# A decoder layer on one core: where the second attention's inputs are loaded, how its mask enters the keys, and where its first maxima are formed

## The chip, the core and the metric

The kernel runs on one core of a Trainium2 chip. Its engines are TensorE (PE: matrix products, with PEld for the loading of their weights), VectorE (DVE), ScalarE (ACT), GpSimd (POOL) and SyncE (SP), whose queue here issues nearly all transfers. Each engine runs its own instructions in order, and engines wait for each other at semaphores. The metric is the device time of one execution in microseconds; lower is better.

## What is computed

One decoder layer on x (4 batches of 1024 tokens, 256 channels). Each of the three parts ends in a residual sum and a layer norm. The change is in the second part, the attention over a context of 77 rows for each batch.

```python
x = _layernorm(x + _L0_attn_ref(x, ...))         # attention of x on itself, rotary, alibi
# second part: q = x, k = v = ctx_1024 (4, 77, 256), 16 heads of 16 channels
qh = _split_heads(q @ Wq.T + bq)
kh = _split_heads(k @ Wk.T + bk)
vh = _split_heads(v @ Wv.T + bv)
scores = jnp.einsum('bhqd,bhkd->bhqk', qh, kh) / jnp.sqrt(jnp.float32(HEAD_DIM))
scores = scores + mask.astype(scores.dtype) * NEG          # NEG = -1e15
weights = jax.nn.softmax(scores, axis=-1)
attn = jnp.einsum('bhqk,bhkd->bhqd', weights, vh)          # then @ Wo.T + bo
# third part: a router with 8 experts, two for each token
```

## The kernel before

The program is a row of stages: projections (`stage_qkv`), first attention (`stage_attention`), its output projection with the norm and the second attention's queries (`stage_self_out`, tiles named `so_`), the second attention (`stage_cross`, tiles named `cr_`), router, experts, and the last norm. A stage begins on all engines when all have finished the one before. In a stage every engine has a program of its own, written out by hand in the order in which it runs, and semaphores tie them together. The order is fixed in the code; no planner moves anything.

Numbers are kept precise by splitting a float into two parts (hi and lo, type fp32r) and adding three products (`parts3`).

`stage_self_out` works in 8 chunks of 512 tokens. SP issues all loads first, then, chunk by chunk, the stores of x1 (`store_x1`) and of the two parts of the queries (`store_q`, to `q2_scr`).

`stage_cross` begins with a preparation:

- SP loads context, key weights, masks and constants, then the first stacks of queries. `load_stack(n)` puts the queries of chunk n, which six transfers of 256 KB read from `q2_scr`, into `qst[n % 4]`; it waits until POOL has filled that tile with ones (`pool_done`).
- ScalarE and VectorE split the context and the key weights. The parts lie in `qst[2]` and `qst[3]` (`spare`), so POOL fills these two only when the values' products are done (`turn_full` is 2).
- TensorE forms the keys for 8 pairs of heads (L1656). For each pair there are six products of 128 rows and 308 columns, and two more of one row that add the mask's parts: `mask_row` times `mask_hi` and times `mask_lo`. ScalarE and VectorE turn each result into `k_max` and `k_exp` (`key_exp`, L1380, L1474, L1476).
- Then come the maxima of the scores. A chunk has 8 half steps; `max_pairs(h)` is eight small products into `m_ps` on TensorE (L1588), and `maxima(h)` is one reduction on VectorE (L1493). There is one `m_ps`, so the products of h wait for the reduction of h-1. The first 14 (`LEAD`) run ahead of everything else, with the values' products (L1667) behind h = 1.
- When a chunk's eight maxima are there, `shifts(n)` negates them, `transpose_top(n)` turns them on TensorE, `copy_top(n)` copies them (ScalarE), and `move_top(n)` on SP writes them to `shift_scr` and reads them back into two rows of the query stack (`top_in`). `scores(n, 0)` waits for that. SP's order at the start is `load_stack(0)`, `load_stack(1)`, `load_x(0)`, `load_stack(2)`, `move_top(0)`, `load_stack(3)`, `move_top(1)`.

The main loop then runs over the 8 chunks: in each of a chunk's 8 steps the maxima of a later chunk, the scores of this one, and pieces of values, transposes, projection and norm of this and earlier chunks.

Of the kernel before, what the change touches and what calls it, by code (L numbers as in the profile page):

```python
# [12 lines left out]
F32 = mybir.dt.float32  # L13
# [892 lines left out]
def stage_self_out(nc, io):  # L906

    with Scope(nc, "so") as s:
# [5 lines left out]
        ident = s.sb("ident", [P, P], F32)  # L914
# [35 lines left out]
        def _(sp):  # L950
# [192 lines left out]
L = 77  # L1143
# [46 lines left out]
def stage_cross(nc, io):  # L1190


    with Scope(nc, "cr") as s:
# [7 lines left out]
        ctx = s.sb("ctx", [P, CK, B * L], F32)  # L1201
        wk_raw = s.sb("wk_raw", [P, CK, C], F32)
        wv_raw = s.sb("wv_raw", [P, CK, C], F32)
        bk = s.sb("bk", [P, PAIRS], F32)
        kinds = s.sb("kinds", [P, 3], F32)
        bv = s.sb("bv", [P, C], F32)
        mask_raw = s.sb("mask_raw", [1, P], F32)
        mask_row = s.sb("mask_row", [1, P], F32R)
        mask_i = s.sb("mask_i", [1, B * L], I32)
        mask_f = s.sb("mask_f", [1, B * L], F32)  # L1210
        mask_hi = s.sb("mask_hi", [1, B * L], F32R)
        mask_lo = s.sb("mask_lo", [1, B * L], F32R)
        key_i = s.sb("key_i", [L, B], I32)
        key_bias = s.sb("key_bias", [L, B], F32)
        wo_raw = s.sb("wo_raw", [P, CK, C], F32)
        wo_hi = s.sb("wo_hi", [P, CK, C], F32R)
        wo_lo = s.sb("wo_lo", [P, CK, C], F32R)
        bo = s.sb("bo", [P, C], F32)
        ident = s.sb("ident", [P, P], F32)
# [13 lines left out]
        s_ps = [s.pb(f"s_ps{i}") for i in range(S_BANKS)]  # L1233
# [11 lines left out]
        ctx_in, wv_in = s.sem("ctx_in"), s.sem("wv_in")  # L1245
        const_in, late_in = s.sem("const_in"), s.sem("late_in")
# [24 lines left out]
        def key_bank(j):  # L1271

            banks = [x[:, :] for x in s_ps] + [a_ps[:, :], m_ps[:, 0, :], m_ps[:, 1, :]] + [x[:, :] for x in turn_ps]
            return banks[j][:, 0:B * L]

# [5 lines left out]
        def _(sp):  # L1281
# [35 lines left out]
            sp.dma_start(ctx[:, :, :], io["ctxT"].rearrange("(c p) n -> p c n", p=P)).then_inc(ctx_in, 16)  # L1317
            sp.dma_start(wk_raw[:, :, :], io["wkT"].rearrange("(c p) n -> p c n", p=P)).then_inc(ctx_in, 16)
            sp.dma_start(mask_i[:, :], io["mask"]).then_inc(const_in, 16)
            sp.dma_start(mask_raw[:, :], io["mask_row"]).then_inc(const_in, 16)  # L1320
# [1161 lines left out]
```

## Time and profile before

| | |
|---|---|
| median of 3 runs | 1915.79 us (1911.1 to 1917.71) |
| time of the profiled execution | 1916.35 us |
| its span, first to last instruction | 1914.6 us |
| busy share of the span: PE, DVE, ACT, POOL | 86%, 68%, 52%, 21% |
| mean granted TensorE clock | 0.906 of full |

The profile covers one execution. A busy share is a mean over stages with different limits, so a change in one stage has to be read in that stage: which engine waits there, for whom, and when. A clock of 1.00 is 2.4 GHz and 0.50 is 1.2 GHz. The second attention takes from about 1037 to about 1297 us in this execution.

### The profile page before, as it was taken

The numbers are of one execution on the slowest core, as the hardware profiler recorded it, in microseconds if no ns is written. First come the engines' busy times: TensorE is split into PE (matmuls) and PEld (weight loads), VectorE is DVE, ScalarE is ACT, GpSimd is POOL, SyncE is SP. The second block draws the span as 40 slices with busy tenths as digits, with TensorE's granted clock in tenths as the row PEclk, the third lists the DMA queues.
The fourth block names the chain that finished last, engine by engine and source line by source line (L and its number), as shares of the span: only waits on it lengthen the run. The fifth ranks groups of instructions, "written<-read, shape, count | busy, mean of one in ns | idle before, by whom it ended". The sixth has DMA issues, their size and how long they took to land. (4 is left out here: it accounts for less than half of the span.)

```text
span 1914.6 us, 36288 instructions
## 1 busy us (share of the span) xinstructions
PE 1654.9 (86%) x14824; PEld 1080.1 (56%) x14824; DVE 1296.4 (68%) x2288; ACT 992.3 (52%) x1692; POOL 404.2 (21%) x268
## 2 busy tenths in 40 slices
PE   7858999999999999998584799877993999999970
PEld 7734444444444444443374555545762888988870
DVE  6687888888888888883294446752333777777736
ACT  5324777777777777777342166853442333333310
POOL 6440000000000000000223100000453344444430
PEclk9957999999999999999797567977996999999995
DMA  7877444444444444400546766313213233334225
GB/s 254 218 186 210 63 68 65 66 66 68 67 66 65 69 63 68 64 14 8 182 143 179 111 94 112 80 45 133 90 41 113 67 92 92 92 92 92 37 31 178
DMA packets 131409, 183.93 MB, mean 96 GB/s; under 512 B 30904, under 2 KB 95560, under 8 KB 130188
## 3 DMA queue, kind: packets, MB, share of 16 engines
q1 hardware_dynamic: 117804, 159.56, 39.4%
q0 software_dynamic: 13440, 22.07, 5.5%
q8 instruction: 117, 1.92, 0.5%
q14 instruction: 48, 0.39, 0.1%
HBM read 114.95 MB, written 69.99 MB: 97 GB/s over the span
## 5 line engine op out<-in xcount | busy, mean ns | idle before, releaser
L638 DVE TENSOR_REDUCE att_row_max<-att_ring 128x2 f32<-128x1024 f32 x512 | 602.4, 1220 | 108.0 <-PE att_ring L704 56.9
L622 ACT ACTIVATE att_w_exp<-att_s_ps 128x512 f32<-128x512 f32 x1024 | 547.8, 596 | 231.9 <-PE att_s_ps L747 156.4
L774 PE MATMUL att_a_ps<-att_w_exp,att_v_group 128*32 128x512 f32 x2048 | 273.6, 606 | 0.2 <-ACT att_w_exp L622 0.2
L733 PE MATMUL att_s_ps<-att_q_stack,att_k_stack 62*128 62x512 f32 x640 | 181.5, 480 | 0.0
L733 PEld LDWEIGHTS att_s_ps<-att_q_stack,att_k_stack 62*128 62x128 f32 x640 | 84.3, 184 | 123.9 <-ACT att_w_exp L622 112.8
L2156 ACT ACTIVATE ex_hid<-ex_h_ps,ex_b 128x512 f32<-128x512 f32 x128 | 87.2, 686 | 116.4 <-DVE ex_h_lo L2211 66.6
L2112 POOL DMA_INDIRECT x_scr<-ex_y,ex_home x64 | 106.7, 1666 | 181.4 <-DVE ex_y L2201 166.8
L560 POOL COPY att_eyes<-keep_slope_eye 128x384 bf16<-128x384 bf16 x16 | 8.1, 507 | 641.1 <-PE att_s_ps L747 631.8
L2211 DVE TENSOR_TENSOR ex_h_lo<-ex_hid,ex_h_hi 128x512 fp32r<-128x512 f32 x128 | 138.8, 1085 | 4.4
L704 PE MATMUL att_ring<-att_k_stack,att_q_stack 60*128 60x512 f32 x640 | 131.4, 451 | 6.3 <-DVE att_att L665 3.2
L747 PE MATMUL att_s_ps<-att_eyes,keep_past_bf 64*128 64x64 bf16 x3840 | 133.4, 193 | 0.0
L733 PE MATMUL att_s_ps<-keep_q_stack,keep_k_stack 62*128 62x512 f32 x384 | 114.3, 488 | 8.9 <-ACT att_w_exp L622 6.3
L747 PEld LDWEIGHTS att_s_ps<-att_eyes,keep_past_bf 64*128 64x128 bf16 x3840 | 93.6, 96 | 30.0 <-issue 13.5
L704 PE MATMUL att_ring<-keep_k_stack,keep_q_stack 60*128 60x512 f32 x384 | 89.8, 503 | 22.2 <-DVE att_row_max L638 11.2
L733 PEld LDWEIGHTS att_s_ps<-keep_q_stack,keep_k_stack 62*128 62x128 f32 x384 | 51.6, 188 | 88.9 <-ACT att_w_exp L622 80.3
L1402 ACT ACTIVATE cr_e<-cr_s_ps,cr_key_bias 77x512 f32<-77x512 f32 x128 | 80.3, 679 | 31.1 <-PE cr_s_ps L1608 30.1
L1817 POOL DMA_INDIRECT rows_scr<-ro_x_send,ro_put_u x64 | 64.8, 1013 | 123.3 <-DVE ro_put_u L1930 69.0
L2142 ACT ACTIVATE ex_x_hi<-ex_t_ps 128x1024 fp32r<-128x1024 f32 x16 | 16.4, 1027 | 141.1 <-PE ex_t_ps L2260 141.1
L1493 DVE TENSOR_REDUCE cr_top<-cr_m_ps 128x8 f32<-128x616 f32 x64 | 51.0, 797 | 53.8 <-PE cr_m_ps L1588 53.7
L2209 DVE CAST ex_h_hi<-ex_hid 128x512 fp32r<-128x512 f32 x128 | 72.7, 568 | 14.5 <-ACT ex_hid L2156 13.5
L2219 DVE TENSOR_TENSOR ex_y<-ex_y_ps,ex_b 128x256 f32<-128x256 f32 x64 | 25.4, 421 | 81.8 <-PE ex_y_ps L2283 81.8
L2283 PE MATMUL ex_y_ps<-first_w_hi,ex_h_lo 128*128 128x256 f32 x256 | 72.5, 283 | 0.0
(296 smaller groups left out, 3544.0 us busy)
## 6 DMA issues: line engine op xcount, KB each, us to landing
first_w_raw<-ew SPq DMA_DIRECT2D x16, 1024.0 KB
att_k_stack<-qk_scr SPq DMA_DIRECT2D x120, 128.0 KB
cr_q_stack<-q_scr SPq DMA_DIRECT2D x48, 256.0 KB, 9.3
keep_k_stack<-qk_scr SPq DMA_DIRECT2D x72, 128.0 KB
rows_scr<-att_zeros POOLq DMA_DIRECT2D x8, 1040.0 KB, 22.0
ex_rows<-rows_scr SPq DMA_DIRECT2D x16, 520.0 KB
att_q_stack<-qk_scr SPq DMA_DIRECT2D x60, 128.0 KB
qk_scr<-qkv_t_hi SPq DMA_DIRECT2D x7, 1024.0 KB, 4.3
```

The costliest lines, as they stand in the source:

```text
L622: nc.scalar.activation(w_exp[(STEPS * g.n + st) % SETS][h][:, :], s_ps[v % BANKS][:, :], ACT.Exp).then_inc(exp_done, 1)
L638: nc.vector.tensor_reduce(out, ring[place.slot][:, :, :], AX.X, ALU.max).then_inc(ring_free, 1)
L704: return nc.tensor.matmul(ring[place.slot][:, i, :], qs[g.buf][rows, j, tok:tok + P], ks[g.buf][rows, half, j, kk * CH:(kk + 1) * CH], sta ...
L733: ins = nc.tensor.matmul(s_ps[v % BANKS][:, :], ks[g.buf][rows, c, j, kt * P:(kt + 1) * P], qs[g.buf][rows, j, c * CH:(c + 1) * CH], start ...
L747: ins = nc.tensor.matmul(s_ps[bank][:, at:at + 64], past[side, far, half, :], eyes[g.buf][side, part, h // 2, :], start=False, stop=n == last)
L774: ins = nc.tensor.matmul(a_ps[32 * h:32 * h + 32, :], vg[g.buf][:, kt, h * VW:h * VW + 32], w_exp[(STEPS * g.n + st) % SETS][h][:, :], sta ...
L1402: nc.scalar.activation(e[p % E_SETS][:, side, :], s_ps[v % S_BANKS][0:L, :], ACT.Exp, bias=key_bias[:, n // 2:n // 2 + 1]).then_inc(exp_do ...
L2112: pool.indirect_dma_start(io["x2_scr"], bass.IndirectOffsetOnAxis(home[h % 4][:, t, :], 0), y[c][:, t, :], None, compute_op=ALU.add).then_ ...
L2156: nc.scalar.activation(hid[m % 2][:, :], h_ps[m % 2][:, :], ACT.Relu, bias=b1[:, bass.ds(e, 1), m:m + 1].rearrange("p a b -> p (a b)") if ...
L2209: nc.vector.tensor_copy(h_hi[c][:, m, :], hid[m % 2][:, :]).then_inc(h_hi_done, 1)
L2211: nc.vector.tensor_tensor(h_lo[c][:, m, :], hid[m % 2][:, :], h_hi[c][:, m, :].bitcast(F32), ALU.subtract).then_inc(h_lo_done, 1)
L2283: ins = nc.tensor.matmul(y_ps[t][:, 0:C], a, b, start=(j == 0), stop=(j == len(prods) - 1))
```

## The change

There are three edits.

1. A scope `pre` holds context, weights, biases, masks, constants and the identity for both stages. `load_cross` issues their 11 transfers in `stage_self_out`, behind the loads of that stage's eighth chunk and ahead of its first store. `stage_cross` issues none of them (it issued twelve), and waits for one semaphore, `cross_in`.
2. `mask_hi` and `mask_lo` become one tile of 64 rows, `mask_parts`: the high part in row 0, the low part in row 32, zeros elsewhere, as in `mask_row`. The two products of one row become one of 64 rows.
3. The first 14 maxima alternate between `m_ps` and the first two score banks (`max_bank`), and wait for the reduction two before.

```diff
@@ stage_self_out, SP
             for n in range(1, CHUNKS):
                 load(n)
+            load_cross(sp, io, pre)
             for n in range(CHUNKS + 2):
@@ new
+def load_cross(sp, io, pre):
+
+    for tile, name in (("ctx", "ctxT"), ("wk_raw", "wkT"), ("wv_raw", "wvT"), ("wo_raw", "woT")):
+        sp.dma_start(pre[tile][:, :, :], io[name].rearrange("(c p) n -> p c n", p=P)).then_inc(pre["cross_in"], 16)
+    for tile, name in (("bk", "bk_stack"), ("kinds", "kinds"), ("mask_raw", "mask_row"), ("mask_i", "mask"), ("key_i", "maskT")):
+        sp.dma_start(pre[tile][:, :], io[name]).then_inc(pre["cross_in"], 16)
+    for name in ("bv", "bo"):
+        sp.dma_start(pre[name][:, :], io[name].partition_broadcast(P)).then_inc(pre["cross_in"], 16)
@@ stage_cross
-        s_ps = [s.pb(f"s_ps{i}") for i in range(S_BANKS)]
+        score_ps = s.pb("score_ps", (P, S_BANKS, 512))
+        s_ps = [score_ps[:, i, :] for i in range(S_BANKS)]
+        def max_bank(h):
+
+            return score_ps[:, 0:2, :] if h < LEAD and h % 2 else m_ps[:, :, :]
@@ SP
-            sp.dma_start(ctx[:, :, :], io["ctxT"].rearrange("(c p) n -> p c n", p=P)).then_inc(ctx_in, 16)
...
             load_stack(0)
-            sp.dma_start(wv_raw[:, :, :], io["wvT"].rearrange("(c p) n -> p c n", p=P)).then_inc(wv_in, 16)
-            sp.dma_start(bv[:, :], io["bv"].partition_broadcast(P)).then_inc(wv_in, 16)
-            sp.dma_start(ident[:, :], io["ident"]).then_inc(late_in, 16)
             load_stack(1)
-            sp.dma_start(bo[:, :], io["bo"].partition_broadcast(P)).then_inc(late_in, 16)
-            sp.dma_start(wo_raw[:, :, :], io["woT"].rearrange("(c p) n -> p c n", p=P)).then_inc(late_in, 16)
             load_x(0)
@@ VectorE
-            nc.vector.tensor_copy(mask_hi[:, :], mask_f[:, :]).then_inc(prep, 1)
+            nc.vector.tensor_copy(mask_parts[:, :], mask_f[:, :]).then_inc(prep, 1)
             dve.wait_ge(prep, 7)
-            nc.vector.tensor_tensor(mask_lo[:, :], mask_f[:, :], mask_hi[:, :].bitcast(F32), ALU.subtract).then_inc(prep, 1)
+            nc.vector.tensor_tensor(mask_parts[32:64, :], mask_f[32:64, :], mask_parts[32:64, :].bitcast(F32), ALU.subtract).then_inc(prep, 1)
@@ TensorE
-                if h:
+                if 2 <= h < LEAD:
+                    pe.wait_ge(m_free, h - 1)
+                elif h >= LEAD:
                     pe.wait_ge(m_free, h)
-                prods += [(mask_row[:, :], x[:, :]) for x in (mask_hi, mask_lo)]
+                prods.append((mask_row[:, :], mask_parts[:, :]))
```

The next two lists are TensorE's rows at the end of the key products and the start of the maxima, before and then after. `q_stack` here stands for the split context and weights, which lie in that tile's memory; each row gives the result's shape and the number of like instructions.

```order
L1656 MATMUL cr_turn_ps<-cr_q_stack 128x308 x6
L1656 MATMUL cr_turn_ps<-cr_mask_hi,cr_mask_row 128x308
L1656 MATMUL cr_turn_ps<-cr_mask_lo,cr_mask_row 128x308
L1588 MATMUL cr_m_ps<-cr_k_max,cr_q_stack 128x78 x16
L1667 MATMUL cr_turn_ps<-cr_q_stack 77x256 x24
L1588 MATMUL cr_m_ps<-cr_k_max,cr_q_stack 128x78 x56
L1597 MATMUL cr_turn_ps<-cr_ident,cr_neg 32x128 x4
```

```order
L1666 MATMUL cr_turn_ps<-cr_q_stack 128x308 x6
L1666 MATMUL cr_turn_ps<-cr_mask_parts,cr_mask_row 128x308
L1598 MATMUL cr_m_ps<-cr_k_max,cr_q_stack 128x78 x8
L1598 MATMUL cr_score_ps<-cr_k_max,cr_q_stack 128x78 x8
L1677 MATMUL cr_turn_ps<-cr_q_stack 77x256 x24
L1598 MATMUL cr_m_ps<-cr_k_max,cr_q_stack 128x78 x8
L1598 MATMUL cr_score_ps<-cr_k_max,cr_q_stack 128x78 x8
```

Each pair of heads has one product less, and the groups of eight maxima products now alternate between two tiles. The order of the groups is the same.

The next two lists are SP's rows at the start of the second attention, before and then after. In the kernel before, seven loads (context, key weights, masks, constants) stand ahead of the first row.

```order
L1292 DMA cr_q_stack<-q_scr 16x8x512 x6
L1325 DMA cr_wv_raw<-wvT 128x2x256
L1326 DMA cr_bv<-bv 128x256
L1327 DMA cr_ident<-ident 128x128
L1292 DMA cr_q_stack<-q_scr 16x8x512 x6
L1329 DMA cr_bo<-bo 128x256
L1330 DMA cr_wo_raw<-woT 128x2x256
L1299 DMA cr_x<-x_scr 128x4x256
L1292 DMA cr_q_stack<-q_scr 16x8x512 x6
L1304 DMA shift_scr<-cr_neg_t 32x512
L1308 DMA cr_q_stack<-shift_scr 2x4096 x2
```

```order
L1315 DMA cr_q_stack<-q_scr 16x8x512 x12
L1322 DMA cr_x<-x_scr 128x4x256
L1315 DMA cr_q_stack<-q_scr 16x8x512 x6
L1327 DMA shift_scr<-cr_neg_t 32x512
L1331 DMA cr_q_stack<-shift_scr 2x4096 x2
```

The weights and constants are gone from this place, and the third stack still stands ahead of the write to `shift_scr`.

## Rows read from the trace of the kernel before

**Rows 1.** The page's first line: span and instructions.

```profile
span 1914.6 us, 36288 instructions
```

**Rows 2.** Busy time in one stretch: PE, PEld, DVE, ACT, POOL, PEclk, DMA share, GB/s.

```profile
1050.00:1055.00 5.00, 5.00 (x16) 3.76 (x16) 0.00 (x0) 0.00 (x0) 0.00 (x0) 0.50 1.07 122
```

**Rows 3.** Timeline (start, length, engine, line, operation): SP's loads and stores, then stage_cross.

```profile
952.17 1.42 SPq L953 DMA_DIRECT2D so_x<-x  x1
...
964.17 0.37 SPq L957 DMA_DIRECT2D x_scr<-so_x  x1
...
1042.06 0.80 DVE L1451 TENSOR_TENSOR cr_q_stack<-cr_ctx,cr_q_stack 128x616 fp32r<-128x616 f32 x1 [1.11 <-ACT cr_q_stack L1362]
...
1046.45 1.88 PE L1656 MATMUL cr_s_ps<-cr_q_stack 128*128 128x308 f32 x6 [18.65 <-DVE cr_mask_row L1467]
```

**Rows 4.** Timeline, TensorE, the second key product, then the first maxima product.

```profile
1049.07 0.63 PE L1656 MATMUL cr_s_ps<-cr_q_stack 128*128 128x308 f32 x1
...
1049.49 0.97 PE L1656 MATMUL cr_s_ps<-cr_q_stack 128*128 128x308 f32 x3
...
1050.51 0.46 PE L1656 MATMUL cr_s_ps<-cr_q_stack 128*128 128x308 f32 x1
...
1050.90 0.62 PE L1656 MATMUL cr_s_ps<-cr_mask_hi,cr_mask_row 1*128 1x308 f32 x1
...
1051.71 0.63 PE L1656 MATMUL cr_s_ps<-cr_q_stack 128*128 128x308 f32 x1
...
1069.48 1.08 PE L1588 MATMUL cr_m_ps<-cr_k_max,cr_q_stack 52*128 52x78 f32 x8 [1.82 <-DVE cr_k_max L1476]
```

**Rows 5.** Timeline, TensorE, maxima products and what follows them.

```profile
1088.16 1.07 PE L1588 MATMUL cr_m_ps<-cr_k_max,cr_q_stack 52*128 52x78 f32 x8 [0.98 <-DVE cr_top L1493]
...
1089.17 1.03 PE L1597 MATMUL cr_turn_ps<-cr_ident,cr_neg 128*32 128x128 f32 x4
...
1100.64 1.07 PE L1588 MATMUL cr_m_ps<-cr_k_max,cr_q_stack 52*128 52x78 f32 x8 [1.55 <-DVE cr_wo_lo L1538]
...
1101.49 0.72 PE L1608 MATMUL cr_s_ps<-cr_q_stack,cr_k_exp 50*77 50x512 f32 x2
```

**Rows 6.** Timeline, the maxima before and behind the values' products.

```profile
1071.45 1.08 PE L1588 MATMUL cr_m_ps<-cr_k_max,cr_q_stack 52*128 52x78 f32 x8 [0.89 <-DVE cr_top L1493]
...
1077.02 0.64 PE L1588 MATMUL cr_m_ps<-cr_k_max,cr_q_stack 52*128 52x78 f32 x8
...
1087.22 0.80 DVE L1493 TENSOR_REDUCE cr_top<-cr_m_ps 128x8 f32<-128x616 f32 x1 [1.17 <-PE cr_m_ps L1588]
```

**Rows 7.** Timeline of POOL and SP's queue, one busy stretch, transfers' landing (last: shift_scr's).

```profile
1077.15 6.97 POOL L1350 MEMSET cr_q_stack<- 128x4096 f32 x2 [32.85 <-PE cr_turn_ps L1667]
...
1080.69 2.70 SPq L1292 DMA_DIRECT2D cr_q_stack<-q_scr  x6
...
1090.85 0.31 SPq L1304 DMA_DIRECT2D shift_scr<-cr_neg_t  x1
...
1096.18 0.54 SPq L1308 DMA_DIRECT2D cr_q_stack<-shift_scr  x2
...
1093.00:1094.00 1.00, 0.18 (x2) 0.03 (x2) 0.78 (x1) 0.00 (x0) 0.00 (x0) 0.50 0.66 72
...
cr_wv_raw<-wvT SPq DMA_DIRECT2D x1, 256.0 KB, 12.8
...
DMA to landing us min/median/max: 1.6/3.7/7.0
```

**Rows 8.** Timeline, ScalarE, copy_top of successive chunks; busy time in two stretches.

```profile
1150.34 0.59 ACT L1393 ACTIVATE cr_neg_t<-cr_turn_ps 32x512 fp32r<-32x512 f32 x1 [1.50 <-PE cr_turn_ps L1597]
...
1178.46 0.59 ACT L1393 ACTIVATE cr_neg_t<-cr_turn_ps 32x512 fp32r<-32x512 f32 x1 [1.70 <-PE cr_turn_ps L1597]
...
1198.84 0.59 ACT L1393 ACTIVATE cr_neg_t<-cr_turn_ps 32x512 fp32r<-32x512 f32 x1 [1.49 <-PE cr_turn_ps L1597]
...
1165.00:1170.00 5.00, 5.00 (x31) 2.43 (x28) 1.50 (x3) 2.77 (x5) 0.00 (x0) 0.50 1.08 144
```

More of the change, by code:

```diff
@@ L903, in chunk_rows, with cross_tiles, stage_self_out @@
     return ap.rearrange("(n t p) e -> n p t e", p=P, t=TPC)[n]
-def stage_self_out(nc, io):
+CROSS_LOADS = 11
+MASK_ROWS = 64
+def cross_tiles(s):
+    shapes = {"ctx": [P, CK, B * L], "wk_raw": [P, CK, C], "wv_raw": [P, CK, C], "wo_raw": [P, CK, C], "bk": [P, PAIRS],
+              "bv": [P, C], "bo": [P, C], "kinds": [P, 3], "mask_raw": [MASK_ROWS, P], "ident": [P, P]}
+    pre = {name: s.sb(name, shape, F32) for name, shape in shapes.items()}
+    pre["mask_i"], pre["key_i"] = s.sb("mask_i", [MASK_ROWS, B * L], I32), s.sb("key_i", [L, B], I32)
+    pre["cross_in"] = s.sem("cross_in")
+    return pre
+def load_cross(sp, io, pre):
[5 more added lines that the diff above has]
+        sp.dma_start(pre[name][:, :], io[name].partition_broadcast(P)).then_inc(pre["cross_in"], 16)
+L = 77
+def stage_self_out(nc, io, pre):
     with Scope(nc, "so") as s:
@@ L1187, with stage_cross @@
 TURNS = turns()
[L1190 removed]
+def stage_cross(nc, io, pre):
     with Scope(nc, "cr") as s:
@@ L1271, in key_bank @@
         def key_bank(j):
-            banks = [x[:, :] for x in s_ps] + [a_ps[:, :], m_ps[:, 0, :], m_ps[:, 1, :]] + [x[:, :] for x in turn_ps]
+            banks = s_ps + [a_ps[:, :], m_ps[:, 0, :], m_ps[:, 1, :]] + [x[:, :] for x in turn_ps]
             return banks[j][:, 0:B * L]
+        def max_bank(h):
+            return score_ps[:, 0:2, :] if h < LEAD and h % 2 else m_ps[:, :, :]
         def exp_lag(p):
@@ L1587, in max_pairs @@
                         rows = slice(64 * side, 64 * side + ROWS_MAX)
-                        ins = nc.tensor.matmul(m_ps[:, side, j * LP:(j + 1) * LP], q[rows, first + j, t * P:(t + 1) * P],
+                        ins = nc.tensor.matmul(max_bank(h)[:, side, j * LP:(j + 1) * LP], q[rows, first + j, t * P:(t + 1) * P],
                                                k_max[rows, first + j, b, :], start=True, stop=True)
@@ L2367, in consts @@
         "kinds": kinds.astype(f),
-        "mask_row": mask[None, :].astype(f),
+        "mask_row": padded_rows(mask[None, :].astype(f)),
         "before": (a[:, None] < a[None, :]).astype(f),
@@ L2386, in stacked_bk, with padded_rows @@
     return out.reshape(P, PAIRS)
+def padded_rows(a):
+    out = np.zeros((MASK_ROWS, a.shape[1]), a.dtype)
+    out[::MASK_ROWS // 2] = a
+    return out
 def padded_rw2(w):
@@ L2400 @@
     "ctxT": ("ctx_1024", lambda a: a.reshape(B * L, C).T),
-    "mask": ("mask_Bx1x1xS2_ik0", lambda a: a.reshape(1, B * L)),
+    "mask": ("mask_Bx1x1xS2_ik0", lambda a: padded_rows(a.reshape(1, B * L))),
     "maskT": ("mask_Bx1x1xS2_ik0", lambda a: a.reshape(B, L).T),
@@ L2455, in build @@
             stage_attention(nc, io, keep)
-        stage_self_out(nc, io)
-        stage_cross(nc, io)
+        with Scope(nc, "pre") as c:
+            pre = cross_tiles(c)
+            stage_self_out(nc, io, pre)
+            stage_cross(nc, io, pre)
         with Scope(nc, "first") as w:
```

47 lines of the change are left out of this document (13 added, 34 removed).

## The prediction

> **What bounds the kernel now.** I read the page first for its span [rows 1]. The profiled execution took 1916.35 us, 1.75 us more than that span, and lies 0.56 us above the median of the runs shown. I take the sum from 1916.35 us and carry it over to the median. The page's chain of waits covers only the last norm, so it says nothing of the second attention. There I read the timeline engine by engine, then the busy time in short stretches, then the transfers.
>
> The reader should see four things. First, in the key products TensorE is busy 5.00 us of 5.00, at half clock [rows 2]: this phase is bound by TensorE. Second, in the first maxima TensorE and VectorE take turns: from one group of eight products to the next are 1.97 us (1069.48 to 1071.45), with 0.89 us of TensorE waiting for VectorE [rows 4, 6]. Third, the first scores run at 1101.49, right behind the fifteenth maxima, which waited 1.55 us for the low part of the output weights [rows 5]. Fourth, the stage has another chain towards those scores. POOL fills `qst[2]` when the values' products are done, SP then loads that stack, and the write of the first maxima to `shift_scr` stands behind it in the same queue [rows 7].
>
> **The start of the stage.** VectorE waited 1.11 us for ScalarE's part of the context, which waited for the load [rows 3]. With the load done in the stage before, that wait goes. VectorE's own steps (fills, splits, mask) then follow without a gap, so TensorE's first key product moves from 1046.45 to 1045.34: **1.11 us**. The mask steps keep their 308 columns on 64 rows in place of one, which I cost at nothing, since a wider partition range adds no columns. ScalarE's later wait for the value bias goes too; it caught up before the last key, so I give it nothing.
>
> **The moved transfers.** By their shapes they are 1.33 MB (308 KB, three times 256, two times 128, five small ones), in 11 transfers. SP issued the last load of `stage_self_out` at 952.17 and the first store at 964.17, 10.6 us after that load's issue ended [rows 3]. The slowest rate in the rows is 256 KB in 12.8/6 = 2.1 us (the six stack transfers ahead of the value weights, [rows 7]), which would make 5.2 x 2.13 = 11.1 us. So they fit or push the first store by about 1 us, and the first to wait for that store is VectorE two chunks later. I take 0. If that cover were gone, at most these 11.1 us would come back once. Five issues fewer ahead of the second stack matter little: stack 0 waits for POOL's fill anyway.
>
> **The mask product.** One pair of heads takes 1051.71 - 1049.07 = 2.64 us [rows 4]. Between full products the distance is (1050.51 - 1049.49)/4 = 0.255 us. The first one takes 0.42 (1049.07 to 1049.49), the sixth 0.39, and the two products of one row 0.81 together (1050.90 to 1051.71). So one row costs no less than 128, and each change of height costs about 0.15 at either side. Removing one product removes at least 0, if the one of 64 rows took the whole 0.81. It removes 0.855 if it fits in like a full one. Which of the two is it nearer to? Eight maxima products of 52 rows take 0.85 us when the scores of 50 rows follow (1100.64 to 1101.49), but 1.01 when transposes of 128 rows follow (1088.16 to 1089.17) [rows 5]. So a product of half height pays the change as the one-row product does. I take one streaming time, 0.255 us for each pair: 8 x 0.255 = **2.04 us**. The first maxima product moves from 1069.48 to 1066.33.
>
> **The two places.** h = 1 starts 0.86 us behind h = 0 rather than 1.97, so it gives **1.11 us** more, and the values' products follow. The maxima behind them start at 1077.02 - 4.26 = 1072.76 [rows 6]. Two groups then share a cycle of 1.97 us, 0.985 each, so the reduction of h = 7 ends near 1072.76 + 5 x 0.985 + 1.9 = 1079.6, against 1088.02 (87.22 + 0.80) before: 8.4 us earlier [rows 6]. h = 14 and the output weights' low part would let the scores go near 1087.3, or 14.2 us earlier. That is what the maxima alone would give.
>
> **What is late next.** The scores also need the maxima's round trip. POOL's fill of `qst[2]` hangs on the values' products, so it moves only by 4.26 us, from 1077.15 to 1072.9 [rows 7]. The third stack's loads go from 1080.69 to 1076.4. Before, their traffic ended inside 1093 to 1094 (0.66 busy), and the write issued at 1090.85 had landed by 1096.18. The value weights, issued right behind six such transfers, landed 12.8 us after their issue: the queue is served in order. Now the write is issued near 1082.4, 8.4 us earlier, but six transfers that end near 1089.4 are ahead of it. It lands at 1096.18 - 4.26 = 1091.9. The read back then takes between 1.6 us (the least of these transfers' landings [rows 7]) and 5.3 (before, the scores started that long after its issue [rows 5, 7]). I take 2.7 us, an estimate nearer to the least, as the queue is then empty; the median is 3.7 with stacks in the way. Scores start near 1094.6 in place of 1101.49: **6.9 us** earlier, with ends of 4.3 and 8.0. On SP, the third and fourth stack and every later round trip stand behind this wait. They move by 4.3 us or more and were not late before. On TensorE, everything of the main loop is queued behind the scores. So about 7 of the 14 us are lost in a wait for `top_in`, some 7 us long.
>
> Sum: 1916.35 - 6.9 = 1909.4 us, or 1908.9 on the median's basis; I say 1909.
>
> **Rivals.**
>
> *A product of 64 rows is free of the change of height.* It saves 0.855 us for each pair, 4.8 us more in all, ahead of the values' products, and so ahead of both chains: 1904.6. For it speaks only that no such product stands among full ones in the trace; against it the 0.16 us of [rows 5]. Chance 0.13.
>
> *The clock rises in the key products.* If it does at the middle, four pairs save 1.2 us each and the values about 1 us: 5.8 us more, 1903.6. Against it, TensorE was busy 5.00 of 5.00 and the granted clock stayed at 0.50, 1.2 GHz [rows 2]; for it, that six products of seven are now full, where it was six of eight. Chance 0.05. The Trainium skill (TensorE: Matmul & The Clock Gate, "What's actually happening") says that the gate follows how busy TensorE has been of late, and that activity releases it. By that rule alone the clock would have risen in this phase already, before the change as behind it; the row disagrees.
>
> *The write does not wait for the third stack.* Then the two places pay in full, 14.2 us: 1902. Against it stands the order seen in [rows 7]. Chance 0.07.
>
> *Slower: the clock in the main loop.* The place is chunks 1 to 4 of the loop. From the second `copy_top` row to the third are 20.4 us; the chunk ahead of it, which holds a stretch at 0.50 with TensorE busy all of it, took 28.1 [rows 8]. One such chunk more costs 7.7 us, and whether the clock rises in a chunk may hang on how its work falls in time, which the change moves. At 0.9 chunk the gain is gone (1909.4 + 6.9), from 1.6 on the kernel is slower by more than 0.3%; two give 1924.8. As easily, the chunk that ran at half before is spared, and the time is 1901.7. The three runs lie within 6.6 us, which speaks against large swings. Chance of slower this way 0.12.
>
> *The change does little.* If the read back takes 5.3 us and the mask product saves nothing, 2.3 us are left: 1914. Chance 0.1.
>
> **How the numbers follow.** The forecast has 0.53. Its own range is 1905 to 1913, by the round trip's ends and part of a clock stretch. About 0.3%, 5.7 us, is what a measurement of this kernel can tell from no change, so the forecast lies just beyond that bound, and some 0.19 of its 0.53 falls inside. The three rivals with larger gains hold 0.25, of which I count 0.24 as faster; the little gain counts as the same. Together: faster 0.58, same 0.30, slower 0.12. The range for 8 in 10 reaches over the other gains to 1901 and over the small gain to 1917.
>
> **What would show it.** Right: TensorE's first key product 1.1 us nearer to the stage's start; 2.39 us for a pair of heads; maxima groups 0.98 us apart; then TensorE idle for about 7 us, ended by the landing of `shift_scr`'s read; the write's landing about 9.5 us after its issue. Wrong: 1.8 us for a pair, a clock of 1.00 before the values, a write that lands within 4 us of its issue, or a chunk of the main loop of 28 us that was of 20.

## The result: 1905.38 us, 0.55% less than before

Over eight executions of each, the changed kernel takes 1905.38 us (median; 1900.54 to 1910.79) and the kernel before 1915.45 (1911.1 to 1918.45). The ratio is 0.9945, with a 95% interval of 0.9927 to 0.9963: a small gain, clear of noise. The forecast was 1909, with a range of 1901 to 1917. The profiled execution took 1905.45 us, against 1916.35: 10.9 us less.

The page of the changed kernel begins with this line, the counterpart of [rows 1]:

```profile
span 1903.6 us, 36270 instructions
```

**Where the 10.9 us are.** In POOL's and SP's timeline (start, length, engine, line, operation), POOL's first fill marks the start of `stage_cross` and SP's first load of the router its end. After the change:

```profile
1040.52 6.96 POOL L1361 MEMSET cr_q_stack<- 128x4096 f32 x2 [4.67 <-POOLq L49]
...
1070.16 6.96 POOL L1361 MEMSET cr_q_stack<- 128x4096 f32 x2 [22.68 <-PE cr_turn_ps L1677]
...
1077.09 2.34 POOL L1368 TENSOR_TENSOR cr_x<-cr_x,pre_bo 128x1024 f32<-128x1024 f32 x1
...
967.60 15.66 SPq L985 DMA_DIRECT2D x_scr<-so_x  x3
...
1073.69 2.67 SPq L1315 DMA_DIRECT2D cr_q_stack<-q_scr  x6
...
1081.25 0.32 SPq L1327 DMA_DIRECT2D shift_scr<-cr_neg_t  x1
...
1090.07 0.54 SPq L1331 DMA_DIRECT2D cr_q_stack<-shift_scr  x2
...
1286.80 0.35 SPq L1798 DMA_DIRECT2D ro_ident<-ident  x1
```

And the same two marks in the kernel before:

```profile
1037.34 6.96 POOL L1350 MEMSET cr_q_stack<- 128x4096 f32 x2 [4.68 <-POOLq L49]
...
1297.71 0.35 SPq L1788 DMA_DIRECT2D ro_ident<-ident  x1
```

The stage took 1297.71 - 1037.34 = 260.37 us and takes 1286.80 - 1040.52 = 246.28 now: 14.1 less. It starts 3.2 us later; already the end of the first stage, which the change does not touch, is 2.85 us later in this execution. What follows the stage is alike: 1914.6 - 1297.71 = 616.9 us and 1903.6 - 1286.80 = 616.8. `stage_self_out` did not grow: from its first store of x1 ([rows 3] and 967.60 here) to the stage's start are 73.17 us before and 72.92 now. So its own work hides the 11 transfers.

**Inside the stage**, all times from POOL's first fill. TensorE's timeline of the changed kernel, which answers to [rows 4 to 6]:

```profile
1049.32 1.88 PE L1666 MATMUL cr_score_ps<-cr_q_stack 128*128 128x308 f32 x6 [18.33 <-DVE cr_mask_row L1475]
...
1051.68 1.91 PE L1666 MATMUL cr_score_ps<-cr_q_stack 128*128 128x308 f32 x6
...
1054.07 1.91 PE L1666 MATMUL cr_score_ps<-cr_q_stack 128*128 128x308 f32 x6
...
1058.63 1.12 PE L1666 MATMUL cr_m_ps<-cr_q_stack 128*128 128x308 f32 x6
...
1060.01 1.12 PE L1666 MATMUL cr_m_ps<-cr_q_stack 128*128 128x308 f32 x6
...
1066.04 0.64 PE L1598 MATMUL cr_m_ps<-cr_k_max,cr_q_stack 52*128 52x78 f32 x8 [1.82 <-DVE cr_k_max L1484]
...
1066.51 0.62 PE L1598 MATMUL cr_score_ps<-cr_k_max,cr_q_stack 52*128 52x78 f32 x8
...
1067.06 3.04 PE L1677 MATMUL cr_turn_ps<-cr_q_stack 128*77 128x256 f32 x24
...
1070.02 0.64 PE L1598 MATMUL cr_m_ps<-cr_k_max,cr_q_stack 52*128 52x78 f32 x8
...
1087.10 1.07 PE L1598 MATMUL cr_m_ps<-cr_k_max,cr_q_stack 52*128 52x78 f32 x8 [1.55 <-DVE cr_wo_lo L1546]
...
1094.90 0.71 PE L1618 MATMUL cr_score_ps<-cr_q_stack,cr_k_exp 50*77 50x512 f32 x2 [6.73 <-DMA cr_q_stack<-shift_scr]
```

| | before | after | change |
|---|---|---|---|
| first key product | 9.11 | 8.80 | -0.31 |
| first maxima (h = 0) | 32.14 | 25.52 | -6.62 |
| maxima of h = 2, behind the values | 39.68 | 29.50 | -10.18 |
| write of the first maxima issued | 53.51 | 40.73 | -12.78 |
| first scores | 64.15 | 54.38 | -9.77 |
| end of the stage | 260.37 | 246.28 | -14.09 |

One pair of heads takes 1054.07 - 1051.68 = 2.39 us at first; at 1058.63 its six full products take 1.12 us in place of 1.91, and the whole pair 1060.01 - 1058.63 = 1.38. Busy time in stretches (length, PE, PEld, DVE, ACT, POOL, clock, DMA share, GB/s) shows why, beside [rows 2]:

```profile
1050.00:1055.00 5.00, 5.00 (x16) 3.84 (x16) 1.40 (x3) 1.04 (x2) 0.00 (x0) 0.50 1.05 127
...
1060.00:1065.00 5.00, 4.22 (x22) 3.14 (x21) 4.06 (x8) 3.61 (x8) 0.00 (x0) 1.00 1.06 132
```

TensorE is busy 5.00 of 5.00 as before, and the granted clock goes from 0.50 (1.2 GHz) to 1.00 (2.4 GHz) inside the key products. In the kernel before it stayed at 0.50 through all of them and rose only in the values' products.

VectorE has two surprises, its cast of the mask and the two steps of `shifts(0)`, which negate the first maxima. The first line is a step that is as quick as before:

```profile
1044.01 0.76 DVE L1459 TENSOR_TENSOR cr_q_stack<-pre_ctx,cr_q_stack 128x616 fp32r<-128x616 f32 x1
...
1046.48 1.17 DVE L1467 CAST cr_mask_f<-pre_mask_i 64x308 f32<-64x308 int32 x1
...
1070.80 0.79 DVE L1501 TENSOR_REDUCE cr_top<-cr_m_ps 128x8 f32<-128x616 f32 x1
...
1074.58 0.79 DVE L1501 TENSOR_REDUCE cr_top<-cr_score_ps 128x8 f32<-128x616 f32 x1
...
1075.41 1.76 DVE L1508 TENSOR_SCALAR cr_neg<-cr_top 128x64 fp32r<-128x64 f32 x1
...
1077.20 2.30 DVE L1510 SCALAR_TENSOR_TENSOR cr_neg<-cr_top,cr_neg 128x64 fp32r<-128x64 f32 x1
```

The same steps before the change:

```profile
1044.61 0.30 DVE L1459 CAST cr_mask_f<-cr_mask_i 1x308 f32<-1x308 int32 x1
...
1088.05 0.19 DVE L1500 TENSOR_SCALAR cr_neg<-cr_top 128x64 fp32r<-128x64 f32 x1
...
1088.28 0.23 DVE L1502 SCALAR_TENSOR_TENSOR cr_neg<-cr_top,cr_neg 128x64 fp32r<-128x64 f32 x1
```

The six reductions of h = 2 to 7 now follow each other (1070.80 to 1074.58, 0.76 us each, against a cycle of 1.97 before [rows 4, 6]). But `shifts(0)` takes 4.09 us from its first step's start to its second's end, in place of 0.46.

Behind the scores the loop is the same code, yet it takes 191.90 us in place of 196.22. Two successive `copy_top` rows of ScalarE's timeline, beside [rows 8]:

```profile
1124.50 0.59 ACT L1401 ACTIVATE cr_neg_t<-cr_turn_ps 32x512 fp32r<-32x512 f32 x1 [1.73 <-PE cr_turn_ps L1607]
...
1150.42 0.59 ACT L1401 ACTIVATE cr_neg_t<-cr_turn_ps 32x512 fp32r<-32x512 f32 x1 [1.50 <-PE cr_turn_ps L1607]
```

These are the third and fourth, 25.9 us apart. The chunk of 28.1 us in [rows 8] lay one later; that place takes 20.4 us now.

### The profile page after: what moved, and what is told of

It reads as the page before. It is cut to its first block and busy times, and to the rows that moved or that the text cites. A ratio compares the mean times of both kernels' runs of the same rounds, so it can differ in the third digit from the quotient of the medians.

```text
span 1903.6 us, 36270 instructions
## 1 busy us (share of the span) xinstructions
PE 1637.1 (86%) x14816; PEld 1066.9 (56%) x14816; DVE 1302.4 (68%) x2288; ACT 993.9 (52%) x1692; POOL 403.4 (21%) x268
## 5 line engine op out<-in xcount | busy, mean ns | idle before, releaser
L704 PE MATMUL att_ring<-keep_k_stack,keep_q_stack 60*128 60x512 f32 x384 | 89.8, 503 | 22.2 <-DVE att_row_max L638 11.2
L1410 ACT ACTIVATE cr_e<-cr_score_ps,cr_key_bias 77x512 f32<-77x512 f32 x128 | 80.3, 678 | 30.0 <-PE cr_score_ps L1618 29.1
L1501 DVE TENSOR_REDUCE cr_top<-cr_m_ps 128x8 f32<-128x616 f32 x57 | 45.4, 797 | 45.6 <-PE cr_m_ps L1598 45.3
L1846 ACT ACTIVATE ro_hid<-ro_h_ps,ro_rb 128x512 f32<-128x512 f32 x64 | 44.0, 687 | 60.5 <-PE ro_h_ps L1980 60.5
```

The lines of the kernel that those rows point to most:

```text
L704: return nc.tensor.matmul(ring[place.slot][:, i, :], qs[g.buf][rows, j, tok:tok + P], ks[g.buf][rows, half, j, kk * CH:(kk + 1) * CH], sta ...
L1410: nc.scalar.activation(e[p % E_SETS][:, side, :], s_ps[v % S_BANKS][0:L, :], ACT.Exp, bias=key_bias[:, n // 2:n // 2 + 1]).then_inc(exp_do ...
```

## The experiments

Three sets of four kernels ran, each set beside the kernel before on the same chip. A ratio is to that. The points in time in the table come from one profiled execution of each kernel and are again from the stage's start; "trip" is from the issue of the write of the first maxima to the first scores.

| kernel | h = 0 | h = 2 | write | scores | trip | scores to end | ratio, 95% |
|---|---|---|---|---|---|---|---|
| before | 32.14 | 39.68 | 53.51 | 64.15 | 10.64 | 196.22 | 1 |
| the changed kernel | 25.52 | 29.50 | 40.73 | 54.38 | 13.65 | 191.90 | 0.9945 |
| again, first set | 28.53 | 35.46 | 46.68 | 59.26 | 12.58 | 196.46 | 0.9927 [0.9900, 0.9954] |
| again, second set | 28.45 | 35.35 | 46.58 | 58.48 | 11.90 | 194.97 | 0.9956 [0.9922, 0.9991] |
| again, third set | 24.34 | 29.83 | 41.05 | 51.85 | 10.80 | 194.70 | 0.9941 [0.9922, 0.9961] |
| mask in two products | 31.71 | 38.90 | 50.12 | 62.31 | 12.19 | 191.88 | 0.9991 [0.9965, 1.0016] |
| one place | 23.38 | 30.84 | 44.67 | 55.46 | 10.79 | 191.41 | 0.9970 [0.9948, 0.9993] |
| one place, repeated | 24.42 | 32.27 | 45.97 | 56.60 | 10.63 | 189.74 | 0.9956 [0.9935, 0.9977] |
| early loads alone | 31.71 | 39.34 | 53.16 | 63.80 | 10.64 | 196.00 | 1.0001 [0.9982, 1.0020] |
| mask product alone | 28.84 | 36.37 | 50.19 | 60.83 | 10.64 | 196.08 | 0.9987 [0.9962, 1.0011] |
| mask added twice | 25.61 | 32.61 | 43.84 | 55.19 | 11.35 | 191.90 | 0.9954 [0.9922, 0.9987] |
| spare tiles swapped | 24.25 | 29.74 | 37.75 | 48.56 | 10.81 | 195.03 | 0.9914 [0.9891, 0.9937] |
| trip on ScalarE's queue | 24.52 | 30.04 | 41.27 | 59.21 | 17.94 | 194.79 | 0.9984 [0.9954, 1.0013] |
| the same, one place | 28.51 | 36.06 | 49.89 | 67.78 | 17.89 | 191.45 | 0.9991 [0.9963, 1.0019] |

**The changed kernel again.** The same code; it also serves as the measure for its set.

> The changed kernel once more. Theory A (the 64-row mask product lets the clock rise in the key products every time): the granted clock goes from 0.50 to 1.00 inside the eight key products here as well, the first maxima product starts 25 to 26 us behind the stage's first instruction, and the time is 10 us below the kernel before. Theory B (the clock rose there by chance of timing): the clock may stay at 0.50 through all key products, first maxima 28 to 29 us behind the stage's start, and the time is some 5 us below the kernel before. In both TensorE waits 6 to 8 us for shift_scr's read ahead of the first scores.

1904.04 us. The clock rose in the key products again, but only 24.8 us behind the stage's start in place of 17.8, which puts h = 0 3 us later (28.53; neither theory had that), and the main loop took 4.6 us more. The profiled execution was the slowest of its seven, 1913.44 us. So the time of the rise and the loop's length are properties of an execution, and differences of 3 to 5 us between two profiles say nothing of the code. The medians and counts over kernels have to.

**The mask in two products of one row**, the rest as changed:

```diff
-        mask_parts = s.sb("mask_parts", [MASK_ROWS, B * L], F32R)
+        mask_hi = s.sb("mask_hi", [1, B * L], F32R)
+        mask_lo = s.sb("mask_lo", [1, B * L], F32R)
...
-                prods.append((mask_row[:, :], mask_parts[:, :]))
+                prods += [(mask_row[0:1, :], x[:, :]) for x in (mask_hi, mask_lo)]
```

> The changed kernel with two mask products of one row as before; loads and two places stay. Theory A: pairs of heads at 2.64 us, clock at 0.50 through all of them, first maxima product 30.5 us behind the stage's start (25.5 in the changed kernel), and since the third stack hangs on it the first scores 5 to 7 us later: time 5 to 7 us above the changed kernel. Theory B: the clock rises or not as in the changed kernel; the time is 2 us above it.

1912.87 us, 8.8 us above the changed kernel of its set, and the two intervals do not touch. TensorE's timeline, first maxima and first scores:

```profile
1070.60 1.07 PE L1599 MATMUL cr_m_ps<-cr_k_max,cr_q_stack 52*128 52x78 f32 x8 [1.82 <-DVE cr_k_max L1485]
...
1101.20 0.71 PE L1619 MATMUL cr_score_ps<-cr_q_stack,cr_k_exp 50*77 50x512 f32 x2 [5.27 <-DMA cr_q_stack<-shift_scr]
```

The clock stayed at 0.50 through the key products, as before, and h = 0 starts 6.2 us later than in the changed kernel. 8 x 0.255 = 2.04 us of this is the shorter work; the rest is the clock.

**One place for the first maxima**, the rest as changed:

```diff
-            return score_ps[:, 0:2, :] if h < LEAD and h % 2 else m_ps[:, :, :]
+            return m_ps[:, :, :]
...
-                if 2 <= h < LEAD:
-                    pe.wait_ge(m_free, h - 1)
-                elif h >= LEAD:
-                    pe.wait_ge(m_free, h)
+                if h:
+                    pe.wait_ge(m_free, h)
```

> The changed kernel with all first maxima in m_ps again; loads and the mask product stay. Theory A (the maxima's round trip through shift_scr sets the first scores): the maxima behind the values' products take 1.5 to 2 us each in place of 0.8 to 1, the 13th ends some 6 to 10 us later, but the scores begin at most 2 to 3 us later, since they waited 6.7 us for the read; time 1 to 3 us above the changed kernel. Rival (the maxima set it): 6 to 10 us above it.

1911.36 us, 7.3 us above the changed kernel of its set: by the medians the rival's figure. In the profiles its scores come only 1.1 us later than in the changed kernel, as theory A has it, so the two measures disagree. Here is TensorE's row of the first scores, which wait for nothing:

```profile
1094.62 0.71 PE L1616 MATMUL cr_score_ps<-cr_q_stack,cr_k_exp 50*77 50x512 f32 x2
```

**Both undone**, so that only the early loads are left:

> The kernel before with the early loads alone (two one-row mask products, one place). My sum: 0.3 to 1.1 us below the kernel before, not to be told from it. Rival (late loads of the value bias and weights held ScalarE and so the keys): 4 us or more below it.

1916.61 us, ratio 1.0001, with an interval of 0.2% to either side: no worth or cost of the early loads alone can be seen.

**The round trip on ScalarE's queue.** `move_top(0)` leaves SP's order; ScalarE issues its write and its read behind `copy_top(0)`. The aim was to take the trip out from behind the third stack.

```diff
             load_stack(2)
-            move_top(0)
...
             copy_top(0)
+            act.wait_ge(top_copied, 1)
+            nc.scalar.dma_start(io["shift_scr"][0], neg_t[0][:, :].bitcast(F32)).then_inc(top_out, 16)
+            act.wait_ge(top_out, 16)
+            for side in range(2):
+                row = 64 * side + ROW_SHIFT
+                nc.scalar.dma_start(qst[0][row:row + 2, :, :].bitcast(F32), ...).then_inc(top_in[0], 16)
```

> The changed kernel, but the first chunk's round trip through shift_scr (one write, two reads) is issued by ScalarE on its own queue, not by SP behind the third stack. Theory A (the trip waits in SP's queue behind the third stack): the read is issued within 4 us of the write (8.2 to 8.8 in the changed kernel), the first scores start 3 to 7 us earlier, then the maxima of step 16 wait for the third stack instead; time 2 to 5 us below the changed kernel. Rival (transfers share the engines whatever the queue, or the maxima set the pace): the read is issued as late as before, time unchanged.

1912.41 us (0.9984 [0.9954, 1.0013]): not to be told from the kernel before, nor, by the intervals, from the changed kernel on the same chip (0.9956 [0.9922, 0.9991]). ScalarE's issues and TensorE's first scores:

```profile
1078.37 0.35 ACTq L1425 DMA_DIRECT2D shift_scr<-cr_neg_t  x1
...
1089.84 0.73 ACTq L1429 DMA_DIRECT2D cr_q_stack<-shift_scr  x2
...
1096.31 0.71 PE L1624 MATMUL cr_score_ps<-cr_q_stack,cr_k_exp 50*77 50x512 f32 x2 [11.02 <-DMA cr_q_stack<-shift_scr]
```

The write took 11.5 us to the read's issue and the read 6.5. SP, no longer held by the trip, issued the twelve transfers of the third and fourth stack one behind the other from 1070.81 on, ahead of the write. So a queue of another engine gave this write no way past twelve transfers: the theory that the order within SP's queue alone makes the write late fell. The run doesn't show what the write would take there with only six ahead.

**The same, with one place.**

> As e5, but with all first maxima in m_ps. Theory A: now that the trip is short, the maxima's own pace shows: first scores 4 to 8 us later than in e5, and no earlier than in e3 by more than 1 us. Rival (the two places are worth little anyway): within 2 us of e5.

1915.35 us (0.9991 [0.9963, 1.0019]), scores at 67.78 against 59.21. The clock rose 9 us later in this profile, which puts h = 0 4 us later (28.51 against 24.52), so only about half of the 8.6 us is the maxima's. The times don't tell the two apart. The write took 12.6 us to the read's issue here.

**The mask added twice**, by two products of 64 rows. This tells "fewer products" from "another height":

```diff
-                prods.append((mask_row[:, :], mask_parts[:, :]))
+                prods += [(mask_row[:, :], mask_parts[:, :])] * 2
```

> The changed kernel with the 64-row mask product done twice for each pair (the mask is added twice). A pair takes 2.64 us at half clock, as in the kernel before. Theory A1 (two products in eight that use few rows kept the clock low): it rises here too, since half the rows are in use, and the first maxima come 24 to 30 us behind the stage's start. Theory A2 (it is the share of full products, six of eight or six of seven): the clock stays at 0.50, first maxima at 31.7 us as with the one-row products, and the time is 4 to 8 us above the changed kernel.

1906.26 us. TensorE's timeline of the key products:

```profile
1049.42 0.88 PE L1666 MATMUL cr_score_ps<-cr_mask_parts,cr_mask_row 64*128 64x308 f32 x2
...
1050.23 1.91 PE L1666 MATMUL cr_score_ps<-cr_q_stack 128*128 128x308 f32 x6
...
1052.88 1.65 PE L1666 MATMUL cr_score_ps<-cr_q_stack 128*128 128x308 f32 x6
...
1056.45 1.11 PE L1666 MATMUL cr_m_ps<-cr_q_stack 128*128 128x308 f32 x6
...
1064.42 1.07 PE L1598 MATMUL cr_m_ps<-cr_k_max,cr_q_stack 52*128 52x78 f32 x8 [1.82 <-DVE cr_k_max L1484]
```

A pair takes 1052.88 - 1050.23 = 2.65 us at half clock, as much as before with one-row products (2.64 [rows 4]), and six of its eight products are full, as before. Yet the clock rose: its six full products take 1.65 us in the third pair and 1.11 in the fifth. So the share of full products doesn't decide it, and the rows in the two mask products do. The work of a pair is no shorter here than before the change, and still the ratio is 0.9954: that points to the clock, not the spared product, as what the mask edit is worth.

**The changed kernel, second and third time.**

> The changed kernel once more, on the same chip as e5 to e7: clock up inside the key products, first maxima 25 to 29 us behind the stage's start, first scores at 54 to 60 us, waiting 5 to 7 us for the read of shift_scr; 8 to 13 us below the kernel before.

1908.98 us. The clock rose at 24.7 us, and the scores waited 4.98 us for the read.

> The changed kernel as reference on this chip: 8 to 13 us below the kernel before, clock up inside the key products, first scores 54 to 60 us behind the stage's start.

1903.67 us. The clock rose at 14.9 us, and the scores came at 51.85 us, 2 us before the earliest that was expected. SP's queue and TensorE's first scores, the measure for the next kernel:

```profile
1069.34 2.67 SPq L1315 DMA_DIRECT2D cr_q_stack<-q_scr  x6
...
1076.89 0.32 SPq L1327 DMA_DIRECT2D shift_scr<-cr_neg_t  x1
...
1083.71 0.54 SPq L1331 DMA_DIRECT2D cr_q_stack<-shift_scr  x2
...
1087.69 0.71 PE L1618 MATMUL cr_score_ps<-cr_q_stack,cr_k_exp 50*77 50x512 f32 x2 [3.88 <-DMA cr_q_stack<-shift_scr]
```

**The spare tiles swapped.** The parts of context and key weights change places with those of the value weights, so that `qst[2]` comes free with the keys (`k_done`), 7 us before the values are done:

```diff
-        ... for i in (2, 3)]
+        ... for i in (3, 2)]
...
                 if i == 2:
+                    pool.wait_ge(k_done, PAIRS)
+                if i == 3:
                     pool.wait_ge(turn_full, 2)
```

> The changed kernel with the two borrowed stacks exchanged: the split key weights lie in qst[2], context and value weights in qst[3], and POOL fills qst[2] when the key products are done, not when the values' products are. Theory A (the third stack's loads and the round trip behind them set the first scores): the third stack's load is issued some 5 to 7 us earlier relative to the first maxima (as far as the earlier stacks' traffic allows), the read lands and the first scores start 1 to 6 us earlier than in e11, more where the clock rose late; time 1 to 5 us below e11. Rival (the maxima set the pace): no change against e11.

1898.97 us (1894.98 to 1904.01), the fastest of all, 16 us below the kernel before. It is 4.7 us below the changed kernel of its set, with six executions of each and intervals that overlap, so this last step is likely and not certain. The timeline of POOL, VectorE, SP and TensorE:

```profile
1059.08 3.51 POOL L1363 MEMSET cr_q_stack<- 128x4096 f32 x1 [15.53 <-PE cr_turn_ps L1668]
...
1069.93 2.35 POOL L1370 TENSOR_TENSOR cr_x<-cr_x,pre_bo 128x1024 f32<-128x1024 f32 x1
...
1071.70 0.63 DVE L1510 TENSOR_SCALAR cr_neg<-cr_top 128x64 fp32r<-128x64 f32 x1
...
1072.37 0.23 DVE L1512 SCALAR_TENSOR_TENSOR cr_neg<-cr_top,cr_neg 128x64 fp32r<-128x64 f32 x1
...
1062.62 2.79 SPq L1315 DMA_DIRECT2D cr_q_stack<-q_scr  x6
...
1074.34 0.32 SPq L1327 DMA_DIRECT2D shift_scr<-cr_neg_t  x1
...
1080.37 0.54 SPq L1331 DMA_DIRECT2D cr_q_stack<-shift_scr  x2
...
1085.15 0.71 PE L1620 MATMUL cr_score_ps<-cr_q_stack,cr_k_exp 50*77 50x512 f32 x2 [3.89 <-DMA cr_q_stack<-shift_scr]
```

The third stack's load goes out 26.0 us behind the stage's start in place of 33.5, and the scores come 3.3 us earlier, which is what the chain through the third stack had led one to expect. But the rows say that the 3.3 us were won ahead of the trip. The trip takes as long as in its twin (1074.34 to 1085.15 is 10.81 us; 1076.89 to 1087.69 above is 10.80). The write is issued 3.3 us earlier, because `shifts(0)` takes 0.90 us in place of 4.10.

**One place, repeated,** beside its own measure of the changed kernel:

> e3 once more beside the changed kernel. Theory A (round trip sets the first scores, the second place gives only the 1.1 us at h = 1): time within 2 us of e11. Rival (the two places are worth what e3's median said): 4 to 7 us above e11.

1904.53 us against 1903.67: within the noise. The 7 us of the first comparison did not come back. In the profiles its scores come 4.8 us later and its main loop is 5.0 us shorter, so the stage is as long in both (246.34 and 246.55 us). One thing is steady: from h = 0 to the scores it is 32.0 to 32.2 us in all five profiles with one place in which SP makes the trip, and 27.5 to 30.7 in the six with two places in the common order of tiles. The second place thus brings the scores 1.3 to 4.7 us nearer to h = 0.

**The mask product alone,** on the kernel before:

> The kernel before with the mask edit alone. Theory A (the mask product lets the clock rise, and the late value bias then holds ScalarE): the clock rises inside the key products, ScalarE starts its first k_high near 20.6 us behind the stage's start, where the value bias lands, and the eight pairs then take 1.09 us each, so the first maxima come at 29 to 31 us (32.1 before; 23.4 to 28.5 with loads and mask); time 1 to 4 us below the kernel before. Rival (loads do nothing whatever the clock): first maxima at 24 to 29 us and time as in e10.

1911.23 us (0.9987 [0.9962, 1.0011]). ScalarE's split of the value weights, and TensorE's last pair:

```profile
1053.80 0.63 ACT L1369 ACTIVATE cr_q_stack<-cr_wv_raw 128x512 fp32r<-128x512 f32 x1 [12.49 <-DMA cr_bv<-bv]
...
1060.80 1.12 PE L1656 MATMUL cr_turn_ps<-cr_q_stack 128*128 128x308 f32 x6
```

The split waits 12.49 us for the load of the value bias, which this kernel issues in the stage. Even so the clock rose in the key products, at 25.1 us, at the end of the seventh pair, and h = 0 comes at 28.84. The wait for the value bias can hardly be the reason for the late rise: with early loads it came as late in three profiles (24.7 to 24.8 us), with h = 0 at 28.45 to 28.53.

## Why `shifts(0)` and the casts became slow

The timelines, laid side by side, show it. In the changed kernel POOL's second fill ends at 1070.16 + 6.96 = 1077.12, and the first step of `shifts(0)` at 1075.41 + 1.76 = 1077.17. POOL's next step, a sum on `cr_x`, runs from 1077.09 to 1079.43, and the second step of `shifts(0)` ends at 1079.50. The mask's cast ends at 1046.48 + 1.17 = 1047.65 in the profile, just behind POOL's first fill (1047.48). It is so in every one of the fourteen profiles:

| | VectorE's step meets POOL's | VectorE's step comes later |
|---|---|---|
| mask's cast against POOL's first fill | 1.17 or 1.18 us in 12 profiles (all with early loads; it starts 1.0 before the fill's end in each) | 0.30 us in 2 (before, mask product alone; 0.2 to 0.3 behind its end) |
| `shifts(0)`, first and second step, against POOL's second fill and sum | 1.0 to 1.8 and 2.30 us in 7 profiles (two places) | 0.20 and 0.23 us in 6 (one place) |

In the seven, the first step starts 0.95 to 1.72 us before the end of POOL's fill and yet ends 0.04 or 0.05 us behind it each time. The cast always starts at the same distance, so its end alone proves less; but on the same 64 rows it takes 0.30 us in the run with the mask product alone, behind the fill. The swapped kernel lies between: its first step meets only the end of POOL's sum (1069.93 + 2.35 = 1072.28; the step ends at 1072.33), and the second is free. The reductions, which read PSUM, keep their 0.80 us while POOL fills, and so do the splits, which have two inputs in SBUF (0.76 us at 1044.01). So these small steps of VectorE wait inside, without any semaphore, until the running step of POOL is over. The Trainium skill (SBUF — State Buffer, "SBUF: two separate sides") describes this: VectorE and GpSimd share one pair of ports as an exclusive lock, taken by GpSimd's operations and by VectorE's in a two-port mode or with two inputs in SBUF (these only against one of GpSimd that reads SBUF), and the later one is blocked for the whole instruction. The trace agrees in both kinds: the step with one input is held by the fill, the one with two by the sum. No run here moved POOL's steps and nothing else, so the cause is shown by these ends and by the swapped kernel, not by an experiment of its own.

## The prediction, step by step

**The start of the stage: 1.11 us forecast, 0.31 measured.** The wait of VectorE for ScalarE's part went. But the casts, now earlier, ran into POOL's fill and took 0.87 us more (1.17 against 0.30). The wait that was removed uncovered another.

**The moved transfers: nothing forecast, nothing measured** (ratio 1.0001 alone). The stage that now issues them took 72.92 us from its first store, 73.17 before.

**The mask product: the mechanism right, the term mis-sized.** 2.39 us for a pair at half clock is the forecast to the digit, so a product of 64 rows pays for its change of height. But keys to h = 0 shrank by 6.31 us, not 2.04. The rest, some 4.3 us, is the clock, the rival that got a chance of 0.05. A pair at full clock takes 1.38 us, so each saves 1.01 and not the rival's 1.2. The clock rose in the key products in all 11 profiles in which the mask's product has 64 rows, the trip's two variants included, and in none of the 3 with one-row products, at a busy share of 1.00 in both. The argument against it, "the granted clock stayed at 0.50" with TensorE busy 5.00 of 5.00, was drawn from rows with one-row products in them and did not hold for the new form. The stretch from h = 1 to h = 2, with the values' products, took 1077.02 - 1071.45 = 5.57 us [rows 6] and takes 1070.02 - 1066.51 = 3.51 now: another 2.1 us. Together 6.3 us; the rival's own sum was 5.8. This size is that of one execution, a lucky one: in the three repetitions h = 0 came 3.61, 3.69 and 7.80 us earlier than before, in place of 6.62, and the stretch of the values took 6.05, 6.02 and 5.03 us, as the clock fell to 0.50 again, behind TensorE's wait of 1.82 us at the end of the keys, and stayed there for part of it. Only the profile above has it at 1.00 throughout.

**The two places: h = 1 forecast 0.86 us behind h = 0, measured 0.47** (at full clock; 0.87 in the kernel with one-row masks, at half). From h = 2 to the end of h = 7's reduction it was 11.00 us [rows 6] and is 5.35. The forecast of 0.985 us a group was too slow: at full clock VectorE bounds it, at 0.76. But of these 5.65 us, 3.63 go into `shifts(0)` behind POOL; 0.6 come back, as the products of h = 8 run during that wait and no longer ahead of the transposes. So the write is issued 11.2 us behind h = 2 in every kernel with two places in the common order of tiles, in place of 13.83: 2.6 us gained, whatever the clock does in between. The prediction gave 4.1 and had no term for POOL and VectorE in each other's way.

**The round trip: the wait came as forecast, its parts did not.** TensorE waits 6.73 us for the landing of `shift_scr`'s read; forecast was about 7. The write takes 1090.07 - 1081.25 = 8.82 us (forecast 9.5), the read back 1094.90 - 1090.07 = 4.83 (forecast 2.7). In other executions of the same kernel the write takes 6.82 to 8.19 us and the whole trip 10.80 to 12.58. The 5.3 us from the read to the scores in the kernel before was no landing time: its scores waited for the products ahead of them, not for the read. What the third stack costs is 0.8 to 3.6 us: a write issued 11.1 us behind the start of POOL's second fill takes 6.8 to 8.8 us, one issued 13.6 us or more behind it 5.2 to 6.0. The bulk of the trip, some 6 us for a write and 4 to 5 for a read, is there without any stack close ahead. The step that had the write land at 1091.9 and the read back take 2.7 us thus failed in its second half: 2.1 us too little. Its first half took the landing of before, 5.33 us after its issue, for a wait for the third stack and moved it with that stack; but the runs with one place have 5.2 to 6.0 us with no stack close ahead, so that landing was no such wait.

**The sum.** For the scores 6.9 us were forecast, 9.8 measured: 0.8 less from the start, 4.3 and 2.1 more from the clock and 0.4 from h = 1, and 3.1 less behind h = 2, where the trip gave back what the maxima had won (h = 2 to the scores: 24.47 us before, 24.88 now, 23.80, 23.13 and 22.02 in the repetitions). So the scores' 9.8 us are one execution's figure; the repetitions have 4.9, 5.7 and 12.3. The main loop gave another 4.3 us in this profile. They can't be credited to the change: with the changed code the loop takes from 191.9 to 196.5 us. 3.2 of the 4.3 lie behind the eighth `copy_top` row, a piece that takes 58.84 us before and 55.66 now, and 54.94, 58.96 and 58.61 in the repetitions, by whether the clock stands at 0.50 or near 1.00 some 30 us into it. That the change does nothing to the loop isn't shown either: in the three kernels in which the long chunk takes 28.1 us (before, early loads alone, mask product alone) it took 196.0 to 196.2 us, in the eleven others 189.7 to 196.5.

**The rivals.** "A product of 64 rows is free of the change of height" is refuted by 2.39 us. "The write does not wait for the third stack" is half true, see above, and would have gained little, since the trip is long by itself. "Slower by the main loop's clock" did not come, but its sign did: where a chunk of 19.4 us stood, the four profiles of the changed kernel have 25.7 to 31.2, and the fourth, 28.1 before, takes 20.4. One chunk of 24.9 to 31.2 us stands in each of the fourteen profiles; the long one moved and was not doubled. The time came out at 1905.38, just inside the likeliest case's own range (1905 to 1913), and this is in part luck: the 0.05 rival came true, which made the scores earlier than the sum had them, and the start of the stage, POOL's hold on `shifts(0)` and the longer read took back some of it.

**What stays open.** Why the clock rises where it does, early in some executions and late in others of the same code, and why the rows of the mask's product matter to it. What each edit is worth by itself in time: the changed kernel lies below the one with one-row masks by more than their intervals (0.9927 and 0.9991), but against one place it was 7 us once and 0.9 us once. Loads and mask together, with one place, gave 0.9970 and 0.9956, while the loads alone gave 1.0001 and the mask alone 0.9987; why the two together give more than their sum, if it isn't noise, no run shows. And whether the swapped tiles gain by `shifts(0)` alone, or whether the third stack's earlier load was needed to keep the trip at 10.8 us with the write 3.3 us earlier; the two were moved together.

## What to carry to other kernels

When a change removes or reshapes small matmuls in a stretch at half clock, don't take the clock of the old stretch as given for the new one: price the sum at both levels and give the other one a real chance. When a step is moved earlier, look at what the neighbouring engines run at that moment, without any semaphore between them: here two VectorE steps of 0.2 us became 4 us because they came to lie under GpSimd's fill, and in the version that moved the fill they took 0.9 us and the scores came 3.3 us earlier. Before a transfer's landing is read from who starts behind it, check in the chain that this one really waited for it. And before a stretch of one profile is explained, profile the same code again: here h = 0 moved by 4 us, and the stage took 246.3 to 255.7 us, with no change at all.

## What the runs showed of the hardware

- TensorE's granted clock: in a stretch with TensorE busy all the time it stayed at 0.50 for the 20 us of key products with two products of one row in each pair, and rose to 1.00 within it with one or two products of 64 rows, in 11 of 11 profiles against 0 of 3. When in the stretch it rises differs between executions of the same code by some 10 us: 14.9, 17.8, 24.7 and 24.8 us behind the stage's start.
- A small step of VectorE held by a running one of GpSimd shows up as a long duration, not as a wait: 1.76 and 2.30 us in place of 0.19 and 0.23.
- From the issue of a small write to that of the read which waits for it were 6.8 to 8.8 us behind six transfers of 256 KB in SP's queue, 5.2 to 6.0 with these further ahead, and 11.5 and 12.6 us in ScalarE's queue with twelve ahead in SP's.
- A change of product height costs about 0.15 us at either side at half clock also for 64 rows: six full products and one of 64 take 2.39 us, where seven at 0.255 us would take 1.79.
